# A vision-transformer tower on one core: the output projection of attention in two f16 passes, and a new order of sections in the pipelined step

## The reference, cut to what matters

```
qkv = x @ w_qkv.T + b_qkv            # 12 heads of 16
atten = softmax(q k^T * SCALE)
out = atten v                        # the context, 196 x 192 per image
return out @ w_proj.T + b_proj       # the output projection
```

## Time and profile before

| | |
|---|---|
| median of 3 runs | 3163.67 us (3161.35 to 3172.22) |
| the profiled execution | 3159.79 us, span 3158.0 us |
| TensorE busy | 2817.0 us, 89% of the span |
| VectorE, ScalarE, GpSimd busy | 73%, 59%, 46% |
| tokenizer, about | 0 to 340 us |
| attention, first layer mostly, then second | 350 to 1910 us |
| feed-forward part, about | 1913 us to the end |

### The profile page before, as it was taken

How to read it: one execution, slowest core, us unless ns; L and a number is a source line. 1 busy time by engine, 2 the same in 40 slices (tenths; PEclk the granted TensorE clock), 3 DMA queues, 4 the chain that set the end, 5 groups by cost and what they waited for, 6 DMA issues and landing times. The chain is left out here.

```text
span 3158.0 us, 94811 instructions
## 1 busy us (share of the span) xinstructions
PE 2817.0 (89%) x31229; PEld 2144.8 (68%) x31229; DVE 2314.7 (73%) x5357; ACT 1872.1 (59%) x3666; POOL 1443.2 (46%) x2001
## 2 busy tenths in 40 slices
PE   4999379999999999999999985999984999999998
PEld 3888335555555555555555554999983888888887
DVE  4888467777777777777777754777774777777776
ACT  3888245666666666666666654777752444444443
POOL 2777322333333344444444411577774444444444
PEclk8999679999999999999999997999996999999999
DMA  5564245555565666666666644544433444444443
GB/s 140 159 187 128 58 103 140 133 146 148 148 150 148 155 154 162 159 161 163 157 162 161 161 104 119 147 145 142 146 121 98 66 67 67 67 67 66 67 65 49
DMA packets 514472, 393.85 MB, mean 125 GB/s; under 512 B 222432, under 2 KB 487682, under 8 KB 514178
## 3 DMA queue, kind: packets, MB, share of 16 engines
q1 hardware_dynamic: 472514, 338.78, 42.2%
q0 software_dynamic: 38496, 46.38, 8.4%
q10 hardware_dynamic: 3168, 4.82, 0.6%
HBM read 232.59 MB, written 155.42 MB: 123 GB/s over the span
## 5 line engine op out<-in xcount | busy, mean ns | idle before, releaser
L657 DVE TENSOR_REDUCE a_mx<-a_mxp 98x4 f32<-98x784 f32 x768 | 746.2, 972 | 317.4 <-PE a_mxp L806 315.7
L533 ACT ACTIVATE a_pt<-a_st 98x784 f32<-98x784 f32 x768 | 631.6, 822 | 203.9 <-PE a_st L792 202.9
L1558 POOL DMA_INDIRECT out_dram<-f_yo,f_idg x202 | 332.0, 1644 | 415.9 <-DVE f_yo L1892 379.3
L479 POOL TENSOR_TENSOR a_cn<-a_ctxs,a_rec 128x392 f32<-128x392 f32 x192 | 189.7, 1016 | 533.9 <-DMA a_rec<-a_recip 533.9
L1632 ACT ACTIVATE f_hf<-f_bank,f_b1c 128x256 f32<-128x256 f32 x606 | 253.8, 472 | 236.5 <-PE f_bank L878 236.4
L868 PE MATMUL a_pr<-a_pf,a_cn 128*98 128x192 f32 x1536 | 334.4, 348 | 7.3 <-POOL a_cn L479 4.1
L821 PE MATMUL a_pv<-a_pt,a_vp 98*32 98x196 f32 x6144 | 338.1, 338 | 0.7 <-ACT a_ctxs L564 0.5
L806 PE MATMUL a_mxp<-a_kst,a_qst 48*128 48x196 f16 x3072 | 262.0, 248 | 69.2 <-DMA a_kst<-a_qk 50.2
L2048 PE MATMUL f_bank<-f_w2h,f_hh 128*128 x1212 | 298.9, 247 | 13.2 <-DVE f_hl L1876 11.6
L2049 PE MATMUL f_bank<-f_w2h,f_hl 128*128 x1212 | 298.2, 246 | 0.0
L2050 PE MATMUL f_bank<-f_w2l,f_hh 128*128 x1212 | 298.0, 246 | 0.0
(11 more groups left out here) (304 smaller groups left out, 7688.5 us busy)
## 6 DMA issues: line engine op xcount, KB each, us to landing
a_rec<-a_recip SPq DMA_DIRECT2D x256, 147.0 KB, 3.6
t_rows<-in_x_dram SPq DMA_DIRECT2D x84, 392.0 KB, 5.9
a_qst<-a_qk SPq DMA_DIRECT2D x256, 110.2 KB, 3.3
a_kst<-a_qk SPq DMA_DIRECT2D x256, 110.2 KB, 3.1
f_xg<-f_listed SPq DMA_DIRECT2D x101, 264.0 KB, 2.8
a_qk<-a_qkh SPq DMA_DIRECT2D x128, 196.0 KB, 2.8
a_qk<-a_qkl SPq DMA_DIRECT2D x128, 98.0 KB, 2.9
a_qk<-a_qkh SPq DMA_DIRECT2D x128, 98.0 KB, 2.4
```

The source lines that it names most:

```text
L533: act.activation(pt[k % PT][:].rearrange("p j a t -> p j (a t)"), st_ps[0:half_t, :, 0:unit_t], ACT.Exp, scale=sm_scale).then_inc(exp_s, 1)
L657: dve.tensor_reduce(mx[:, a, :, 2 * p:2 * p + 2].rearrange("p q j -> p j q"), mx_ps[0:half_t, :, 0:unit_t].rearrange("p j (q t) -> p j q t ...
L1558: pool.indirect_dma_start(out, bass.IndirectOffsetOnAxis(ap=idg[i % 3][:, t:t + 1], axis=0), yo[i % 3][:, t, :], None, compute_op=ALU.add) ...
```

## The change

- **The projection's operands.** The weights are split into an f16 high part `ph` and an f16 low part `pl`. The context is split too, but within one operand: the 32 partitions of a head now hold its 16 values twice, rows 0 to 15 as the high half and rows 16 to 31 as the low half. The product with `ph` and the product with `pl` are 6 f16 matmuls for each x, and one more, `ones16` with a bias row, adds the bias: 7 f16 matmuls for each x in place of 3 f32 ones. Two x share `pr_ps`, so VectorE adds the residual twice for a unit, 98x384, and not four times 98x192.
- **The values.** `vp` is laid out feature by feature, 12 heads side by side, and its second half is a copy of the first, made by a new transfer on SP (`twice_s`); the last feature stays at 1 and gives the sum in row 31. TensorE's weights for a head are 32 values with a stride of 12.
- **The context.** The sums are taken from row 31, and a new transfer then copies row 15 over row 31 (`dup_s`). GpSimd runs three instructions of 128x1176 in place of three of 128x392: the division to `cf`, `ch` = `cf` times a 0/1 column in f16, and `cn` = `cf` minus `ch` in f16.
- **The order.** Products and copies move to other slots: values to 0 and 1, turned rows to 2 and 3, the projection to 4 and 6 (two x each), the reciprocal to 5, and others by one or two slots.
- **Preparation.** One more transposed block for the bias, the split of the projection's weights, two more constants.

```diff
-        vp = [sb(f"vp{i}", [half_t, 4, heads, 32], F32) for i in range(2)]
+        vp = [sb(f"vp{i}", [half_t, 4, 32 * heads], F32) for i in range(2)]
-        cn = [sb(f"cn{i}", [128, 3, unit_t], F32) for i in range(2)]
+        cf = sb("cf", [128, 3, unit_t], F32)
+        ch = sb("ch", [128, 3, unit_t], F16)
+        cn = [sb(f"cn{i}", [128, 3, unit_t], F16) for i in range(2)]
-        OUTS, NORM, REC = 4, 5, 64
-        ROWS_AT, TURN_AT, VALUES_AT = (9, 11, 6), (3, 5), (1, 2)
-        PROJECT_AT = ((2, 2, 2), (4, 4, 4), (6, 6, 6), (9, 10, 10))
-        HIGH_PART_AT, VALUES_OUT_AT = (4, 6), (1, 2)
-        LOW_PART_AT, LOW_ROWS_AT, OUT_AT = (4, 7), (9, 11, 6), (3, 4, 7, 11)
+        OUTS, NORM, REC = 2, 5, 64
+        ROWS_AT, TURN_AT, VALUES_AT = (9, 11, 6), (2, 3), (0, 1)
+        PROJECT_AT = (4, 4, 6, 6)
+        HIGH_PART_AT, VALUES_OUT_AT = (3, 6), (1, 2)
+        LOW_PART_AT, LOW_ROWS_AT, OUT_AT = (4, 7), (10, 11, 6), (4, 8)
-        ROWS_FIRST, PART_FIRST, CONTEXT_FIRST, VALUES_FIRST = (1, 1, 0), (0, 1), (1, 1, 1, 1, 1, 1), (0, 0)
-        NEGATED_AT, RECIP_AT, STATS_AT, AGGREGATE_AT = 6, 4, (10, 0), 2
+        ROWS_FIRST, PART_FIRST, CONTEXT_FIRST, VALUES_FIRST = (0, 1, 0), (1, 1), (0, 1, 1, 0, 0, 1), (0, 0)
+        NEGATED_AT, RECIP_AT, STATS_AT, AGGREGATE_AT = 6, 5, (9, 1), 4
...
                     waits(sp,
                           (rec_s, REC * u),
+                          (cn_s, 3 * u - 2),
                           (inv_s, u + 1))
+                    b = (par + 1) % 2
+                    sp.dma_start(ctxs[b][2 * hd - 1::32], ctxs[b][hd - 1::32]).then_inc(dup_s, 16)
                     sp.dma_start(inv_scr[:], inv[:]).then_inc(is_s, 16)
...
                 if "M" in kinds:
+                    u, b = s + 1, (par + 1) % 2
+                    waits(sp,
+                          (pv_s, GROUPS * (u - 1) + 1),
+                          (vp_s, 2 * (u + 1)))
+                    sp.dma_start(vp[b][:, :, dim:2 * dim - heads], vp[b][:, :, 0:dim - heads]).then_inc(twice_s, 16)
                     place_maxima(s + 1, (par + 1) % 2, 0)
...
                     wait(pool, pr_s, OUTS * (u - 1))
+                    wait(pool, cn_s, 3 * u)
+                    wait(pool, dup_s, 16 * (u + 1))
                     wait(pool, rec_s, REC * (u + 1))
-                    for g in range(3):
-                        pool.tensor_tensor(cn[b][:, g, :], ctxs[b][:, g, :], rec[:, g, :], ALU.mult).then_inc(cn_s, 1)
+                    pool.tensor_tensor(cf[:], ctxs[b][:], rec[:], ALU.mult).then_inc(cn_s, 1)
+                    pool.wait_ge(cn_s, 3 * u + 1)
+                    pool.tensor_tensor(ch[:], cf[:], low_half[:].unsqueeze(2).to_broadcast([128, 3, unit_t]), ALU.mult).then_inc(cn_s, 1)
+                    pool.wait_ge(cn_s, 3 * u + 2)
+                    pool.tensor_tensor(cn[b][:], cf[:], ch[:], ALU.subtract).then_inc(cn_s, 1)
...
-                dve.scalar_tensor_tensor(out=xo[b][:, x, :], in0=pr_ps[0:half_t, 0:dim], scalar=1.0 / WSCALE,
-                                         in1=xres[b][:, x, :], op0=ALU.mult, op1=ALU.add).then_inc(xo_s, 1)
+                dve.scalar_tensor_tensor(out=xo[b][:, 2 * x:2 * x + 2, :], in0=pr_ps[0:half_t, 0:2 * dim].rearrange("p (t d) -> p t d", t=2),
+                                         scalar=1.0 / (WSCALE * WSCALE), in1=xres[b][:, 2 * x:2 * x + 2, :],
+                                         op0=ALU.mult, op1=ALU.add).then_inc(xo_s, 1)
...
-                if g6 % 3 == 0:
-                    wait(pe, vp_s, 2 * u + a + 1)
+                if g6 == 0:
+                    wait(pe, twice_s, 16 * (u + 1))
...
-                        ins = pe.matmul(pv_ps[32 * h4:32 * h4 + 32, 0:tok], vp[b][:, 2 * a + kt, h, :], pt[(first + h4) // 2 % PT][:, h4 % 2, kt, :],
+                        ins = pe.matmul(pv_ps[32 * h4:32 * h4 + 32, 0:tok], vp[b][:, 2 * a + kt, :].rearrange("p (c h) -> p c h", h=heads)[:, :, h], pt[(first + h4) // 2 % PT][:, h4 % 2, kt, :],
...
-            def project(u, b, x, g, layer):
-                if g == 0:
-                    wait(pe, xo_s, OUTS * u + x)
+            def project(u, b, x, layer):
+                if x % 2 == 0:
+                    wait(pe, xo_s, OUTS * u + x // 2)
                 if x == 0:
-                    wait(pe, cn_s, 3 * u + g + 1)
-                ins = pe.matmul(pr_ps[0:half_t, 0:dim], cn[b][:, g, x * half_t:(x + 1) * half_t], pf[layer][:, g, :],
-                                start=(g == 0), stop=(g == 2))
-                if g == 2:
+                    wait(pe, cn_s, 3 * (u + 1))
+                ts, at = slice(x * half_t, (x + 1) * half_t), x % 2 * dim
+                ins = products(pe, pr_ps[0:half_t, at:at + dim],
+                               [(ones16[:], pl[layer][:, 3, :])]
+                               + [(cn[b][:, g, ts], w[layer][:, g, :]) for g in range(3) for w in (ph, pl)])
+                if x % 2 == 1:
                     ins.then_inc(pr_s, 1)
```

More of the change, by code:

```diff
@@ L561, in context @@
                 a, g = g6 // 3, g6 % 3
[L562 removed]
+                wait(act, cn_s, 3 * (u - 2) + 1)
                 wait(act, pv_s, GROUPS * u + g6 + 1)
@@ L600, in prepare @@
                 dve.wait_ge(p_ok[layer], done + 2)
-                dve.tensor_reduce(praw[layer][:, :, :, hd + 1:hd + 2], pbv[:], AX.X, ALU.add).then_inc(p_ok[layer], 1)
+                dve.tensor_copy(praw[layer][:, :, :, hd:2 * hd], praw[layer][:, :, :, 0:hd]).then_inc(p_ok[layer], 1)
+                for part in range(2):
+                    dve.tensor_reduce(pbias[layer][:, :, 32 * part:32 * part + 1], pbv[:].rearrange("p e h d -> p e (h d)"),
+                                      AX.X, ALU.add).then_inc(p_ok[layer], 1)
                 dve.wait_ge(w_f[layer], G_READY[layer])
```

80 lines of the change are left out of this document (51 added, 29 removed).

## The result

The changed kernel takes **3270.63 us** in the median of four runs (3258.80 to 3286.84), the kernel before 3166.29 us (3161.35 to 3172.22): ratio **1.0321**, 95% interval [1.0270, 1.0373]. The forecast was 3200 us in a range of 3125 to 3245: slower, as it said, but by 104 us and not by 38.

The account below looks back on a forecast made before the run. SP's in-order issue list was taken as the bound, as close to the step as TensorE. 30 steps at +0.04 and 30 at +0.95 us plus 8 once gave +38, with 2 for the median 3200 us, range 3125 to 3245.

Parts of the forecast that it names:

- at 87% I expect none: TensorE's clock: a fall where it has gaps was named as a risk, none expected at 87% busy.
- the 282 KB: The doubling transfer's bytes, ahead of the first maxima in the same queue: 1.1 us at 250 GB/s.
- a ring of 21.9 us: Loop from SP's stores through the maxima, TensorE's scores, ScalarE and VectorE back: 13.0 plus 8.9 us, within SP's time.
- two more issues on SP: Duplication 0.76 us and doubling 0.87 us with spacing and waits: +1.63 us a step, between 1.1 and 1.9.
- SP's own work: SP's step without its idle wait for QK2's low part: 21.07 us in layer 0, 22.05 in layer 1.
- SP's list as the bound of the full-clock step: SP issues in order and sets the step: 22.70 us in layer 0, 23.68 in layer 1.
- TensorE's saving of 2.1 us a step: Projection: f16 matmuls replace 4.6 us of f32 work a step; no gain if SP sets the step.
- The reciprocal: Moved to slot 5, ready about a us before SP stands at it; cost nothing, covered by SP.
- GpSimd's three passes: Context division and split, 1176 elements each: 9.1 us; their ring of 22.7 us added nothing to the forecast.
- the rival: Slow strided weight loads for the weighted sums: decides from about three times today's duration, 3355 us, chance 0.09.
- The order: Moves of products and copies to other slots: cost nothing, covered by SP; otherwise a few tenths a step.
- Once only: Layer preparation on VectorE, one more transpose and copy, and the end of the kernel: +8 us in all.

Follow-up runs that it names:

- e15: e13 with the first maxima of the next step issued ahead of the four rec transfers; 3265.66 us, ratio 1.0375.
- e17: e13 with twelve unused f16 matmuls (1.19 us) put into TensorE's wait for the keys; ratio 0.9883 to the kernel before.
- e9: The changed kernel with the doubling transfer moved to the end of SP's step, same count of issues; 3244.20 us, ratio 1.0187.
- e2: The kernel before with only the two new transfers and their waits added on SP, on buffers nobody reads; 3273.71 us, ratio 1.0347.
- e11: The changed kernel with ScalarE writing the values twice, so no doubling transfer; the duplication stays on SP; 3202.47 us, ratio 1.0038.
- e13: e11 with the duplication issued from ScalarE's list, so SP issues what it does in the kernel before; ratio 1.0046.
- e4: The changed kernel with GpSimd's second and third pass cut to 24 of 1176 elements, without the context split; ratio 1.0331.
- e16: e15 with twelve unused f16 matmuls (1.19 us) put into TensorE's wait for the keys; 3226.54 us, ratio 1.0129.
- e3: The changed kernel with the old slots for everything but the projection and its residual; 3350.31 us, ratio 1.0594.
- e10: The kernel before with three of SP's issues (rows, residual, output) moved to ScalarE's list; 3314.20 us, ratio 1.0390.
- e5: The changed kernel with 24 unused f16 matmuls (2.14 us) in front of each step's first scores; ratio 1.0330.
- e18: The kernel before with twelve unused f16 matmuls put into TensorE's wait for the keys; ratio 1.0035.
- e1: The changed kernel with both new transfers issued from ScalarE's list in place of SP's; 3199.12 us, ratio 1.0121.

## Why the prediction was wrong in size

**The failed step is the last sentence of the prediction's part on the profile after: "at 87% I expect none."** It names the risk, a granted clock that falls where TensorE has gaps, and sets it to zero. TensorE's busy share came out at 87% of the span as forecast, and 34 of 57 steps ran at a lower clock. That is 49 of the 96.8 us. The share of the span was the wrong row to read; the pauses of a step were the right one. The kernel before has one of 0.5 to 1.2 us in nearly every steady step, the changed kernel one of 1.0 to 2.3 for the maxima and in most steps a second for the keys, and in the steps shown the longer matmuls begin right at or after such a pause. The Trainium skill (TensorE: Matmul & The Clock Gate, "A second HAM failure mode: psum-queue depth-cycling") says that small frequent pauses between groups of matmuls are enough to make the clock go to and fro; the traces of the changed kernel, e15 and e17 agree, and e9 shows that not every such pause does it.

What brought the new pause was in the prediction too, and was waved through: the 282 KB "in front of `place_maxima`", put at 1.1 us in a ring of 21.9 us that "fits inside". It did fit, for the length of a full-clock step; but it left TensorE idle for 1.36 us in front of the first scores, and that is where it costs, by way of the clock. e9 shows that: the transfer at another place of the list, and some 40 us are gone, though TensorE waits for the maxima no less in all.

**The term that was mis-sized: two more issues on SP, "+1.63 us a step".** Full-clock steps are 1.83 us (22.9 - 21.07) and 1.90 us (23.95 - 22.05) longer than SP's own work before. The duplication was right: 0.60 us of issue, and 0.7 with what it waits for, against 0.76. The doubling was taken from the `sums` transfer at 0.62 and took 0.93 us, with its wait 1.19 against 0.87 (from the first `rec` to the maxima 721.43 - 718.26 = 3.17 us, in the earlier trace rows 1023.63 - 1021.65 = 1.98). Summed over the steps that gives 47 us where the prediction had 29.7. With the mechanism right, this alone would have been a miss of 17 us, inside the range.

**What was right.** SP's list as the bound of the full-clock step: e2 makes a loss of this size with it alone, and e11 shortens the step by about what it takes off it. In e13, where the list is that of the kernel before, it no longer is the only bound. SP's wait for the low part of QK2, 23.9 and 10.2 us in the earlier trace rows, is 4.9 us in 5 waits and 1.1 us in 2. TensorE's saving of 2.1 us a step was real (two blocks of 1.29 us in place of four of 1.15, so 2.0) and useless as long as SP set the step; in e17 the steps are 0.85 and 0.38 us shorter than before. The first scores waiting longer for `a_mrow`: 21.8 us in 16 waits against 3.8 in 10.

**Neither here nor there.** The reciprocal, put at ready a us before SP stands at it, held SP for 3.7 us in 6 waits of the window 636 to 976. GpSimd's three passes were put at 9.1 us and take 2.67 + 2.15 + 2.42 = 7.2; TensorE has no wait for `a_cn` in the window 636 to 976, and e4 shows no time that hangs on the second and third. It would be next in line: waits for `a_cn` appear in e15 and e16, where the rest is out of the way. The strided weight loads:

```profile
L863 PEld LDWEIGHTS a_pv<-a_pt,a_vp 98*32 98x32 f32 x1360 | 48.1, 152 | 19.2 <-issue 14.5 <-ACT a_pt L563 1.0
```

The mean of 152 ns has the loads at the lower clock in it; at full clock one takes 144 ns, against 109 in the earlier trace rows. That agrees in direction with the 16-byte rule that the prediction cited from the Trainium skill (SBUF — State Buffer, "Door 1: The DMA port swizzle"), but a group of matmuls still takes 0.91 us; the rival needed three times 109. The order was taken at nothing and is worth some 80 us in the changed kernel (e3). "Once only" was put at 8 us; outside the stretch of steps the profiles differ by 2.0 us.

**What stays open.** The split into 47 and 49 us comes from the lengths of steps in one profile each. That the clock hangs on the pause for the keys is shown by filling it (e13 to e17, e15 to e16). The filling shortens a pause and adds matmuls at once, and no run separates the two. Why one step with two pauses is slow and the next with the same two is not, the runs do not tell: in the changed kernel steps 19 to 20 keep the full clock with pauses of 1.3 to 1.6 and 0.5 to 1.0 us, the slow steady steps of e13 have a single recorded pause, of 1.0 to 1.8 us, while others with one of 1.0 to 1.2 keep the clock, and in e9 and e10 steps with pauses of up to 2.5 us keep it. Nor is it settled why fewer slow steps saved nothing in e5.

## What to carry to other kernels

Work taken off TensorE is only worth something if another engine or queue doesn't set the step, and it may cost: the pauses that it leaves can bring the granted clock down, so look at each step's pauses, their place and its clock, not at the busy share. Price a new transfer by three things: its issue on the list that issues it (by a row of the same shape), its bytes in front of whatever lands next, and who pauses for that. Where a pause can't be removed, unused matmuls that just fit in it can be what makes the optimisation pay; they did in e17, not in e5 or e18.

## What the hardware showed that I had not expected

- Adding 1.19 us of matmuls a step raised the granted clock of the window 700 to 900 from 0.88 to 0.98 (e15 to e16) and from 0.96 to 1.00 (e13 to e17), and the second of these made the kernel 1.6% faster against its own kernel before (1.0046 to 0.9883).
- SP takes 0.93 us to issue one transfer from SBUF to SBUF of 98 partitions with four pieces of 720 bytes, 0.60 us for one of 4 partitions, and 0.35 us for a load of 98 partitions from DRAM.
- Issuing large transfers from ScalarE's list did not take them out of the way of those that SP issues: in e1 a wait of TensorE's moved from slot 0 to slot 6, in e10 it grew to 1.5 to 3.4 us.
- In e9 TensorE waited as long in all as in the changed kernel (24.0 and 21.8 us for the maxima in the same window), with its pauses at other places, and the clock there stayed at 1.00 in 19 steps of layer 0 that follow each other.
- A VectorE instruction on 98x24 elements takes 0.19 us, or 2.15 us when GpSimd began a pass just before it (794.36 and 794.39 above, both 2.15 us long). In e4, without the long passes, its longest of 17 is 0.37 us. The Trainium skill (SBUF — State Buffer, "Who interferes with whom") tells of a lock that GpSimd shares with some kinds of VectorE's instructions, this one's kind among them, and that the later one waits for; the rows agree.
